# The weighing of the second attention's tiles, issued in two halves of 256 columns

## The chip, the cores and the metric

One core of a Trainium2 chip runs the whole program in one launch. The metric is the device time of that launch in microseconds (us). Six names stand for its engines in the profile: PE is the matmul engine and PEld its weight loads, DVE is VectorE, ACT is ScalarE, POOL is GpSimd and SP is SyncE, which issues the DMAs.

## The reference

The input is one sequence of 2048 tokens of 128 features. Four layers follow each other, each added to the stream after a layer norm: a windowed attention with a few global tokens, a memory lookup with a gate, a second attention, and a feed-forward layer with two chosen experts. The change is in the second attention alone:

```
q, k, v = heads of (x @ W.T + b)          # 16 heads of 8 features
q, k = rope(q, k)
scores = einsum('bhnd,bhmd->bhnm', q, k) / sqrt(8)
out = einsum('bhnm,bhmd->bhnd', softmax(scores), v)
```

In the reference the sequence counts as batch 1 here, so that each of the 16 heads has 2048 x 2048 scores.

## The kernel before

The second attention is `attn1_block`. A head is worked off in 16 steps (NT = 16), one for each tile of 128 keys, and a step has NC = 4 chunks of 512 queries. The loop `for s in range(STEPS): step(s)` runs over 16 x 16 = 256 steps, t = s % 16 being the step within its head. PE does three things in a step.

- **Scores** (`scores(c)`, L1090): one matmul of 64 rows by 512 columns for each chunk c. Its contraction takes partitions 0 to 63 for even heads and 64 to 127 for odd ones. Each result takes one of three PSUM banks in turn (TURNING), and waits in `free_bank` until ACT has read the score that was three before it. In the last head the ring has seven banks, since the banks of the row maxima are then free. ACT turns each result into `pb` (L1170, an exponential of 512 columns).
- **Row maxima of a later head** (`rows(g, n)`, L1053): one matmul of the same shape for each chunk, 64 + 12 units ahead of the scores. In steps 0 to 12 of a head this is the next head, which lies in the other half of the partitions; in steps 13 to 15 it is the head after next, in the same half as the scores. The matmuls fill four banks as two pairs, and DVE reduces each pair with one instruction (L1132, 1024 columns). The first matmul of a pair waits until DVE has reduced the pair that was there before:

```
if n % 2 == 0 and g * HALVES + u >= 2:
    pe.wait_ge(rows_reduced, g * HALVES + u - 1)
```

- **Weighing** (`weigh(h, t)`, L1078): the tile whose scores were made two steps earlier is multiplied with its values. The four chunks go to four groups of 32 output partitions of one bank (A_B), and work beside each other. Values and exponentials are float32, and the profile has two matmul records for each of the four. The bank collects the 16 tiles of a head, ACT then saves it as `acc` (L1161).

With S for a score, R for a row matmul and W for the weighing, the order that PE gets in a step is S0 R0 R1 S1 W S2 R2 S3 R3. R0 and R1 are one pair for DVE, R2 and R3 the other. In step 14 of a head the maxima of the next head are transposed right after W (L1068). The rows end at step 237 of 256, since the last head's maxima are complete there. PE issues in this order; where scores and rows lie in different halves of the partitions, their matmuls can run beside each other.

Of the kernel before, what the change touches and what calls it, by code (L numbers as in the profile page):

```python
# [17 lines left out]
NT = N // P  # L18
BANK = 512
NC = N // BANK  # L20
# [14 lines left out]
H1, HD1 = 16, 8  # L35
# [4 lines left out]
VCOLS = 32  # L40
# [883 lines left out]
def attn1_block(nc, m, a):  # L924

    SCALE = HD1 ** -0.5
    with ExitStack() as ctx:
        def sb(name, shape, dt=F32):
            return ctx.enter_context(nc.sbuf_tensor(name, shape, dt))

        def sem(name):
            return ctx.enter_context(nc.semaphore(name))
# [3 lines left out]
        VB = 3  # L936
        qf, kf = m.qf, m.kf
        vx = sb("vx", [P, VB, NT, VCOLS])
        pb = sb("pb", [P, 3, NC, BANK])
# [11 lines left out]
        st_ready, exp_ready, av_done = sem("st_ready"), sem("exp1_ready"), sem("av_done")  # L951
# [3 lines left out]
        M_B, A_B = 0, 6  # L955
        MAXIMA = (0, 1, 2, 3)
        TURNING = (4, 5, 7)
        UNITS = NT * NC
        HALVES = 2 * NT
        LEAD = 12  # L960
        STEPS = H1 * NT
        LOAD = 16 * 2 * PARTS
# [3 lines left out]
        def group(h):  # L966

            return h % 2 * HALFP

        def slot(h):  # L970
            return h // 2 % SLOTS

        def load_count(h):

            return (LOAD if h % 4 else 0) + (h // 4) * (LOAD + 16)
# [4 lines left out]
        def take(use, ring, reader, count):  # L980

            bank = ring[len(bank_of) % len(ring)]
            bank_of[use], freed_by[use] = bank, last_reader.get(bank, (rows_reduced, H1 * HALVES))
            last_reader[bank] = (reader, count)
# [54 lines left out]
        @block.tensor  # L1039
        def _(pe):  # L1040
            def rows(g, n):

                t, c, u = n // NC, n % NC, n // 2
                g0, b = group(g), slot(g)
                if n == 0 and g == 0:
                    pe.wait_ge(m.first_k, 16 * PARTS * NC)
                if g == 0 and n % UNITS_OF_CHUNK == 0:
                    pe.wait_ge(m.first_q[n // UNITS_OF_CHUNK], 16 * PARTS)
                if n == 0 and g:
                    pe.wait_ge(loaded[g % 4], load_count(g))  # L1050
                if n % 2 == 0 and g * HALVES + u >= 2:
                    pe.wait_ge(rows_reduced, g * HALVES + u - 1)
                mm = nc.tensor.matmul(m.psum[:, M_B + (u % 2) * 2 + n % 2, :], qf[g0:g0 + HALFP, b, t * P:(t + 1) * P],  # L1053
                                      kf[g0:g0 + HALFP, b, c * BANK:(c + 1) * BANK], start=True, stop=True)
                if n % 2:
                    mm.then_inc(rows_ready, 1)

            def free_bank(use):
                if freed_by[use]:
                    reader, count = freed_by[use]  # L1060
                    pe.wait_ge(reader, count)
                return bank_of[use]

            def turn_max(g):

                bank = free_bank(("max", g))
                pe.wait_ge(nparts_ready, g + 1)
                nc.tensor.transpose(m.psum[0:PARTS * NT, bank, 0:P], nparts[:, :].bitcast(F32), m.ident[:, :]).then_inc(nT_ready, 1)  # L1068

            def weigh(h, t):  # L1070

                pe.wait_ge(exp_ready, h * UNITS + (t + 1) * NC)
                if t == 0:
                    if h >= 1:
                        pe.wait_ge(acc_saved, h)
                    pe.wait_ge(vx_ready, h + 1)
                for c in range(NC):
                    mm = nc.tensor.matmul(m.psum[c * VCOLS:(c + 1) * VCOLS, A_B, :], vx[:, h % VB, t, :], pb[:, (h * NT + t) % 3, c, :],  # L1078
                                          start=(t == 0), stop=(t == NT - 1))
                mm.then_inc(av_done, 1)  # L1080

            def step(s):

                h, t = s // NT, s % NT
                g0, b = group(h), slot(h)
                if t == 0:
                    pe.wait_ge(max_rows_loaded, (h + 1) * 32)
                def scores(c):
                    bank = free_bank((s, c))
                    nc.tensor.matmul(m.psum[:, bank, :], kf[g0:g0 + HALFP, b, t * P:(t + 1) * P],  # L1090
                                     qf[g0:g0 + HALFP, b, c * BANK:(c + 1) * BANK], start=True, stop=True).then_inc(st_ready, 1)

                for c in range(NC):
                    n = UNITS + LEAD + s * NC + c
                    if c != 1:
                        scores(c)
                    if n < H1 * UNITS:
                        rows(n // UNITS, n % UNITS)
                    if c == 1:
                        scores(c)  # L1100
                        if s >= 2:
                            weigh((s - 2) // NT, (s - 2) % NT)
                        if t == NT - 2 and h + 1 < H1:
                            turn_max(h + 1)

            def keep_clock(g0):

                rows_of = slice(g0, g0 + HALFP)
                nc.tensor.matmul(m.psum[:, A_B if g0 else TURNING[1], :], m.fill[rows_of, 0:P], m.fill[rows_of, :],
                                 start=True, stop=True)  # L1110

            for n in range(UNITS):
                rows(0, n)
                keep_clock(HALFP)
            for n in range(LEAD):
                if n == 8:
                    turn_max(0)
                rows(1, n)
                keep_clock(0)
            for s in range(STEPS):  # L1120
                step(s)
            weigh(H1 - 1, NT - 2)
            weigh(H1 - 1, NT - 1)

        @block.vector
        def _(dve):

            def reduce_rows(v):

                g, u = v // HALVES, v % HALVES  # L1130
                dve.wait_ge(rows_ready, v + 1)
                nc.vector.tensor_reduce(rowmax[:, g % 2, u // 2, u % 2:u % 2 + 1],  # L1132
                                        m.psum[:, M_B + (u % 2) * 2:M_B + (u % 2) * 2 + 2, :].rearrange("p b c -> p (b c)"),
                                        AX_X, ALU.max).then_inc(rows_reduced, 1)

            def save_maxima(g):

                dve.wait_ge(rows_reduced, (g + 1) * HALVES)
                if g >= 1:
                    dve.wait_ge(nparts_ready, g)  # L1140
                nc.vector.tensor_reduce(nfull[:, :], rowmax[:, g % 2, :, :], AX_X, ALU.max, negate=True).then_inc(nmax_ready, 1)  # L1141

            for v in range(H1 * HALVES):
                reduce_rows(v)
# [291 lines left out]
def build(nc, a, out):  # L1436
    with ExitStack() as ctx:
# [61 lines left out]
        with ExitStack() as layer:  # L1499
            def lb(name, shape, dt=F32):  # L1500
                return layer.enter_context(nc.sbuf_tensor(name, shape, dt))

            m.qf, m.kf = lb("qf", [P, 2, N], F32R), lb("kf", [P, 2, N], F32R)
            m.fill = lb("fill", [P, BANK], F32R)
            m.parts = lb("parts", [P, 2, PARTS, N], F32R)
            m.stored = [layer.enter_context(nc.semaphore(f"parts_stored{i}")) for i in range(2)]
            m.first_k = layer.enter_context(nc.semaphore("first_k"))
            m.first_q = [layer.enter_context(nc.semaphore(f"first_q{c}")) for c in range(NC)]
            m.v1, m.attT, m.sums = lb("v1", [P, NT, D]), lb("attT", [P, N]), lb("sums", [P, BANK])
            memory_block(nc, m, a)  # L1510
            m.q_parts = nc.dram_tensor("q_parts", [PARTS, P, N], F32, kind="Internal").ap()
            m.k_parts = nc.dram_tensor("k_parts", [PARTS, P, N], F32, kind="Internal").ap()
            ln_block(nc, m, "ln2")
            project1_block(nc, m, a)
            attn1_block(nc, m, a)
            output1_block(nc, m, a)
# [46 lines left out]
```

## Time and profile before

| what | value |
|---|---|
| median of 3 runs | 1344.07 us (1342.58 to 1347.62) |
| profiled execution, its time | 1344.84 us |
| profiled execution, its span | 1343.1 us |
| mean granted TensorE clock | 0.967 of full speed |
| PE busy | 1267.1 us (94%) |
| DVE busy | 940.0 us (70%) |
| ACT busy | 860.9 us (64%) |
| score matmuls, first and last start | 535.0 and 1211.6 us |

The span reaches from the first to the last instruction of the profiled execution; 1.7 us of its time lie outside it. A busy PE is not a PE at its peak, since matmuls are pipelined and their ends are modelled. For that reason the starts of the matmuls say more than their durations. The second attention takes about half of the span, and it repeats itself: sixteen heads of sixteen steps.

### The profile page before, as it was taken

To read this page: it belongs to the slowest core of one execution; us is meant where nothing else is said; L and a number is where in the kernel's file an instruction comes from. 1 tells how busy PE (TensorE), PEld (TensorE's weight loads), DVE (VectorE), ACT (ScalarE), POOL (GpSimd) and SP (SyncE) were. 2 spreads that over 40 slices of the span, in tenths; PEclk is the share of its full clock that TensorE was granted. 3 is DMA by queue.
4 is the path that set the end of the run, shared out by engine and by line. 5 is a ranking of instruction groups with operands and counts; after the bars stand their busy time and mean duration, and the time that the engine had idled before them with its cause. 6 is when DMAs were issued, how large, how long until landed. Compare 5 with 4: busy or idle time off the path is not lost. (4 is left out here: it accounts for less than half of the span.)

```text
span 1343.1 us, 22401 instructions
## 1 busy us (share of the span) xinstructions
PE 1267.1 (94%) x8112; PEld 724.2 (54%) x8112; DVE 940.0 (70%) x1641; ACT 860.9 (64%) x2402; POOL 189.7 (14%) x365
## 2 busy tenths in 40 slices
PE   5999999999988867999999999999999999995898
PEld 4677777777855533444444444444444444433566
DVE  4566566666658879888888888888888888804200
ACT  1666666666747310777777877877778787792442
POOL 3233333333461120000000000000000000001100
PEclk8999999999998968999999999999999999997899
DMA  3200000000000030000000000000000000000101
GB/s 78 72 9 9 7 4 10 9 1 4 1 2 1 26 134 17 14 20 18 3 19 20 20 11 10 19 20 20 4 17 19 20 3 2 3 3 21 36 1 32
DMA packets 23100, 24.85 MB, mean 18 GB/s; under 512 B 7798, under 2 KB 17910, under 8 KB 21751
## 3 DMA queue, kind: packets, MB, share of 16 engines
q1 hardware_dynamic: 22990, 23.42, 5.5%
q8 instruction: 65, 1.06, 0.3%
q14 instruction: 45, 0.36, 0.1%
HBM read 16.52 MB, written 5.24 MB: 16 GB/s over the span
## 5 line engine op out<-in xcount | busy, mean ns | idle before, releaser
L1132 DVE TENSOR_REDUCE rowmax<-psum 128x1 f32<-128x1024 f32 x512 | 602.1, 1218 | 85.8 <-PE psum L1053 85.6
L1170 ACT ACTIVATE pb<-psum 128x512 f32<-128x512 f32 x1024 | 531.9, 604 | 123.1 <-PE psum L1090 120.1
L1090 PE MATMUL psum<-qf,kf 64*128 64x512 f32 x1024 | 374.1, 441 | 1.5 <-DMA qf<-nT 0.8
L1053 PE MATMUL psum<-kf,qf 64*128 64x512 f32 x1024 | 356.7, 446 | 11.2 <-DVE rowmax L1132 8.5
L1090 PEld LDWEIGHTS psum<-qf,kf 64*128 64x128 f32 x1024 | 171.2, 185 | 273.0 <-ACT pb L1170 252.7
L1078 PE MATMUL psum<-pb,vx 128*32 128x512 f32 x2048 | 273.6, 606 | 0.0
L1053 PEld LDWEIGHTS psum<-kf,qf 64*128 64x128 f32 x1024 | 162.9, 191 | 59.2 <-DVE rowmax L1132 32.8
L528 ACT ACTIVATE pr<-psum,nmax 128x128 f32<-128x128 f32 x256 | 93.7, 366 | 113.3 <-DVE nmax L471 113.2
L566 POOL TENSOR_TENSOR pr<-pr,rtotal 128x256 f32<-128x256 f32 (+1 forms) x256 | 110.5, 452 | 237.1 <-DVE rtotal L479 237.1
L470 DVE TENSOR_REDUCE nmax<-psum 128x2 f32<-128x256 f32 x128 | 53.6, 419 | 63.9 <-PE psum L339 63.1
L1195 POOL CAST nparts<-nfull 128x16 fp32r<-128x16 f32 x16 | 3.1, 197 | 668.0 <-DVE nfull L1141 668.0
L367 PE MATMUL psum<-pt,vz 128*128 128x128 f32 x512 | 78.1, 275 | 0.0
L1078 PEld LDWEIGHTS psum<-pb,vx 128*32 128x32 f32 x2048 | 40.3, 108 | 69.6 <-issue 38.3
L530 ACT ACTIVATE pr<-psum,nmax 128x32 f32<-128x32 f32 x256 | 72.9, 285 | 0.0
L335 PE MATMUL psum<-kx,qs 64*128 64x160 f32 x512 | 69.4, 348 | 1.7 <-ACT pr L530 1.7
L353 PE MATMUL psum<-ident,pr 128*128 128x128 f32 x384 | 70.0, 291 | 1.0 <-POOL pr L566 0.8
L485 DVE COPY pt<-psum 128x384 f32<-128x384 f32 x128 | 67.6, 528 | 1.7 <-PE psum L353 1.5
L367 PEld LDWEIGHTS psum<-pt,vz 128*128 128x128 f32 x512 | 67.5, 192 | 0.0
L335 PEld LDWEIGHTS psum<-kx,qs 64*128 64x128 f32 x512 | 38.6, 184 | 52.7 <-ACT pr L530 39.0
L1376 ACT ACTIVATE hT<-psum,b 128x512 f32<-128x512 f32 x48 | 33.0, 687 | 42.8 <-PE psum L1391 42.6
L530 ACT ACTIVATION_READ_ACCUMULATOR pr<-psum,nmax 128x1 f32 x256 | 52.8, 206 | 0.0
L365 PE MATMUL psum<-pt,gv 128*128 128x128 f32 x256 | 51.2, 282 | 0.3 <-ACT oT L538 0.2
(198 smaller groups left out, 1358.6 us busy)
## 6 DMA issues: line engine op xcount, KB each, us to landing
qf<-q_parts SPq DMA_DIRECT2D x30, 128.0 KB
kf<-k_parts SPq DMA_DIRECT2D x30, 128.0 KB
k_parts<-parts SPq DMA_DIRECT2D x4, 512.0 KB, 3.6
q_parts<-parts SPq DMA_DIRECT2D x4, 512.0 KB, 4.0
cos<-cos_table SPq DMA_DIRECT2D x1, 1024.0 KB, 5.1
sin<-sin_table SPq DMA_DIRECT2D x1, 1024.0 KB, 7.3
attT<-acc SPq DMA_DIRECT2D x64, 16.0 KB
sums<-acc SPq DMA_DIRECT2D x64, 2.0 KB
```

Source lines behind the costliest of these rows:

```text
L335: nc.tensor.matmul(m.psum[:, bank + j, 0:WL], qs[half[j], b, s * P:(s + 1) * P], kx[half[j], b, s, :], start=True, stop=False)
L353: mm = nc.tensor.transpose(m.psum[:, T_B, j * P:(j + 1) * P], pr[:, w % 4, j * P:(j + 1) * P], m.ident[:, :])
L367: mm = nc.tensor.matmul(ob, vz[:, b, j, s, :], pt[:, w % 2, j * P:(j + 1) * P], start=False, stop=(j == 1))
L485: nc.vector.tensor_copy(pt[:, w % 2, :], m.psum[:, T_B, 0:TW]).then_inc(pt_saved, 1)
L528: nc.scalar.activation(pr[:, i % 4, j * P:(j + 1) * P], sc[:, 0:P], ACT.Exp, bias=nmax[:, i % 4, j:j + 1], accum_out=total[:, i % 4, j:j + 1])
L530: mm = nc.scalar.activation(pr[:, i % 4, 2 * P + j * G0:2 * P + (j + 1) * G0], sc[:, P:WL], ACT.Exp, bias=nmax[:, i % 4, 2 + j:3 + j], acc ...
L566: mm = nc.gpsimd.tensor_tensor(prw, prw, rb, ALU.mult)
L1053: mm = nc.tensor.matmul(m.psum[:, M_B + (u % 2) * 2 + n % 2, :], qf[g0:g0 + HALFP, b, t * P:(t + 1) * P], kf[g0:g0 + HALFP, b, c * BANK:(c ...
L1078: mm = nc.tensor.matmul(m.psum[c * VCOLS:(c + 1) * VCOLS, A_B, :], vx[:, h % VB, t, :], pb[:, (h * NT + t) % 3, c, :], start=(t == 0), sto ...
L1090: nc.tensor.matmul(m.psum[:, bank, :], kf[g0:g0 + HALFP, b, t * P:(t + 1) * P], qf[g0:g0 + HALFP, b, c * BANK:(c + 1) * BANK], start=True, ...
L1132: nc.vector.tensor_reduce(rowmax[:, g % 2, u // 2, u % 2:u % 2 + 1], m.psum[:, M_B + (u % 2) * 2:M_B + (u % 2) * 2 + 2, :].rearrange("p b ...
L1170: nc.scalar.activation(pb[:, s % 3, c, :], m.psum[:, bank_of[(s, c)], :], ACT.Exp, scale=SCALE).then_inc(exp_ready, 1)
```

## The change

`weigh` gets a third argument, the part. For tiles 1 to 14 of a head it does columns 0 to 255 of each of the four chunks in part 0, and columns 256 to 511 in part 1. The first and the last tile of a head stay whole and are issued where part 1 is. Part 0 is issued between R0 and R1, part 1 where the whole weighing was. The order of a step is then S0 R0 Wa R1 S1 Wb S2 R2 S3 R3. Since the tile weighed in step t is that of step t - 2, the steps without a Wa are t = 1 and t = 2. The count of finished tiles (av_done) rises with part 1, and the wait for the exponentials stands at part 0.

```diff
+        HALF_B = BANK // 2
...
-            def weigh(h, t):
-
-                pe.wait_ge(exp_ready, h * UNITS + (t + 1) * NC)
+            def weigh(h, t, part):
+
+                whole = t == 0 or t == NT - 1
+                if part == 0 and whole:
+                    return
+                if part == 0 or whole:
+                    pe.wait_ge(exp_ready, h * UNITS + (t + 1) * NC)
                 if t == 0:
                     if h >= 1:
                         pe.wait_ge(acc_saved, h)
                     pe.wait_ge(vx_ready, h + 1)
+                cols = slice(part * HALF_B, (part + 1) * HALF_B) if not whole else slice(0, BANK)
                 for c in range(NC):
-                    mm = nc.tensor.matmul(m.psum[c * VCOLS:(c + 1) * VCOLS, A_B, :], vx[:, h % VB, t, :], pb[:, (h * NT + t) % 3, c, :],
-                                          start=(t == 0), stop=(t == NT - 1))
-                mm.then_inc(av_done, 1)
+                    mm = nc.tensor.matmul(m.psum[c * VCOLS:(c + 1) * VCOLS, A_B, cols], vx[:, h % VB, t, :],
+                                          pb[:, (h * NT + t) % 3, c, cols], start=(t == 0), stop=(t == NT - 1))
+                if part == 1:
+                    mm.then_inc(av_done, 1)
...
                 for c in range(NC):
                     n = UNITS + LEAD + s * NC + c
+                    if c == 1 and s >= 2:
+                        weigh((s - 2) // NT, (s - 2) % NT, 0)
                     if c != 1:
                         scores(c)
...
                     if c == 1:
                         scores(c)
                         if s >= 2:
-                            weigh((s - 2) // NT, (s - 2) % NT)
+                            weigh((s - 2) // NT, (s - 2) % NT, 1)
...
-            weigh(H1 - 1, NT - 2)
-            weigh(H1 - 1, NT - 1)
+            for t in (NT - 2, NT - 1):
+                for part in range(2):
+                    weigh(H1 - 1, t, part)
```

## Rows read from the trace of the kernel before

**Rows 1.** Windows: stretch in us, each engine's busy us and records, clock, DMA share, GB/s

```profile
786.00:829.00 43.00, 42.93 (x262) 19.00 (x258) 37.86 (x34) 34.09 (x67) 0.88 (x4) 1.00 0.05 16
...
1173.00:1214.00 41.00, 40.59 (x233) 14.91 (x232) 0.00 (x0) 38.35 (x76) 0.00 (x0) 1.00 0.01 3
```

**Rows 2.** Waits, 580 to 1160 us: in total us, times, longest us

```profile
PEld psum L1090 <- ACT pb L1170: 218.0, 367, 0.8
ACT pb L1170 <- PE psum L1090: 105.6, 190, 0.8
```

**Rows 3.** Timeline of one step: start us, length us, engine, line, names, count, idle before

```profile
864.07 0.49 PE L1090 MATMUL psum<-qf,kf 64*128 64x512 f32 x1
...
864.40 0.39 PE L1090 MATMUL psum<-qf,kf 64*128 64x512 f32 x1
...
864.40 0.39 PE L1053 MATMUL psum<-kf,qf 64*128 64x512 f32 x1
864.60 2.06 ACT L1170 ACTIVATE pb<-psum 128x512 f32<-128x512 f32 x4 [0.54 <-PE psum L1090]
864.64 0.39 PE L1090 MATMUL psum<-qf,kf 64*128 64x512 f32 x1
...
864.68 0.73 PE L1053 MATMUL psum<-kf,qf 64*128 64x512 f32 x2
864.87 2.36 DVE L1132 TENSOR_REDUCE rowmax<-psum 128x1 f32<-128x1024 f32 x2 [0.24 <-PE psum L1053]
...
865.25 0.49 PE L1090 MATMUL psum<-qf,kf 64*128 64x512 f32 x1
...
865.67 1.07 PE L1078 MATMUL psum<-pb,vx 128*32 128x512 f32 x8
866.66 0.18 PEld L1090 LDWEIGHTS psum<-qf,kf 64*128 64x128 f32 x1 [0.84 <-ACT pb L1170]
866.67 0.49 PE L1090 MATMUL psum<-qf,kf 64*128 64x512 f32 x1
...
867.28 0.73 PE L1053 MATMUL psum<-kf,qf 64*128 64x512 f32 x2
...
867.85 0.49 PE L1090 MATMUL psum<-qf,kf 64*128 64x512 f32 x1
```

**Rows 4.** Timeline of the same step, cut closer so that merged records part

```profile
864.87 1.22 DVE L1132 TENSOR_REDUCE rowmax<-psum 128x1 f32<-128x1024 f32 x1 [0.24 <-PE psum L1053]
865.01 0.39 PE L1053 MATMUL psum<-kf,qf 64*128 64x512 f32 x1
```

**Rows 5.** All instructions of line 1170: min, median, max ns

```profile
L1170 ACT ACTIVATE pb<-psum x1024: 591/598/740, 535.6 to 1212.3; 128x512 f32<-128x512 f32 x171
```

**Rows 6.** Chain that ended last, in the experts: start us, us, count

```profile
1273.55 10.30 PE psum L1391 x24
1283.86 10.72 PE psum L1400 x96
```

**Rows 7.** Timeline of PE, step 13 of a head

```profile
870.07 0.63 PE L1053 MATMUL psum<-kf,qf 64*128 64x512 f32 x2
870.54 0.40 PE L1090 MATMUL psum<-qf,kf 64*128 64x512 f32 x1
870.87 1.07 PE L1078 MATMUL psum<-pb,vx 128*32 128x512 f32 x8
```

**Rows 8.** Timeline of PE in the last head, without row matmuls

```profile
1180.71 1.06 PE L1078 MATMUL psum<-pb,vx 128*32 128x512 f32 x8
1181.70 1.19 PE L1090 MATMUL psum<-qf,kf 64*128 64x512 f32 x4
1182.82 1.06 PE L1078 MATMUL psum<-pb,vx 128*32 128x512 f32 x8
```

**Rows 9.** Timeline of POOL: one such cast in every head

```profile
785.78 0.20 POOL L1195 CAST nparts<-nfull 128x16 fp32r<-128x16 f32 x1 [42.00 <-DVE nfull L1141]
...
828.68 0.20 POOL L1195 CAST nparts<-nfull 128x16 fp32r<-128x16 f32 x1 [41.99 <-DVE nfull L1141]
```

## Prediction

> **What bounds the kernel now.** I read the windows first, to see whether the stage that the change touches has one limit or several. In a stretch of 43 us, one head, PE is busy for 42.9 us, DVE for 37.9 and ACT for 34.1, at the full granted clock; in the last head DVE has nothing to do and PE still fills its time [rows 1]. PE's number is no proof, since its records overlap. The waits are more telling: ACT waits for scores and the scores' weight loads wait for ACT [rows 2]. Two engines that wait for each other form a loop, so the timeline of one step has to say how long each loop is.
>
> The step repeats every 2.60 us: S2 starts at 864.07 and again at 866.67 [rows 3]. Three things take part in it.
>
> - The loop of the exponentials. S2 starts at 864.07, ACT takes it 0.53 later (864.60), needs 0.60 [rows 5], and 0.05 later S1 starts in the bank that this frees (865.25). W follows 0.42 later, the next S2 1.00 after it [rows 3]. That is 0.53 + 0.60 + 0.05 + 0.42 + 1.00 = 2.60, the whole step. This is the binding loop.
> - The loop of the row maxima. R0 starts at 864.68 and R1 at 865.01, 0.33 later [rows 3, 4]. R1 lasts 0.39, DVE could start 0.07 after its end (R3: 864.40 + 0.39 to 864.87) and needs 1.22 [rows 3, 4]. The next R0 comes 0.05 after DVE has ended: 864.87 + 2.36 = 867.23, against 867.28 [rows 3]. R0 to R0 is thus at least 0.33 + 0.39 + 0.07 + 1.22 + 0.05 = 2.06. It has some 0.5 us to spare, which DVE now spends on the pair before.
> - PE alone. S0 to R0, R1 and S1 has one small gap for DVE and one for ACT, so that PE's own pace is close behind both.
>
> **What the change does to a step.** It removes nothing; it adds four matmuls (eight records of weights and eight of matmuls), and moves half of the columns to a place between R0 and R1. No DMA is issued elsewhere, and av_done rises where it did. The added wait for exponentials is met: the tile was finished two steps earlier. Behind it queue R1 and S1, and that is the point.
>
> *Price of a half.* A whole weighing takes 1.00 us from its start to the next score [rows 3], with two records of 512 columns behind each other in each group. The nearest rows for the columns are the float32 matmuls of the experts, 24 records of 512 columns in 10.30 us and 96 of 128 in 10.72 [rows 6]: 0.429 and 0.112 each, 0.83 ns for a column. Twice 256 columns fewer are 0.42 us less, so a half costs 1.00 - 0.42 = 0.58; I take 0.57, as the start of the first group already holds its weight load. The lower bound is 0.43, the columns alone (512 x 0.83 ns); the upper one 0.66, where the fixed part of the whole, 1.00 - 0.85 = 0.15, is half as large again in a half. That a record's length counted for nothing (1.00) is excluded by the experts' rows.
>
> *Price of getting in.* From a late R0 to Wa I take the 0.42 that S1 needs before W, and 0.33 where the matmul in front of it was not late (870.54 to 870.87) [rows 3, 7]. A matmul that follows one of its kind costs 0.23 (864.40 to 864.64) [rows 3].
>
> *Price of getting out.* After W the next matmul lasts 0.49 in place of 0.39, since its weights are loaded only then: load at 866.66, matmul at 866.67 [rows 3]. R1 is now such a matmul. The Trainium skill, page TensorE: Matmul & The Clock Gate, section Step-by-step: what each phase is for, says that the engine pulls weight loads ahead of matmuls in flight where the row groups don't conflict or the load goes to the background buffer. Were that so for R1 behind Wa, 0.10 would fall out of each added switch; the row shows that it is not so behind W.
>
> Now the loop of the maxima is R0, Wa, R1, DVE, R0: 0.42 + 0.57 + (0.49 + 0.07) + 1.22 + 0.05 = 2.82. R1 is 0.66 us later behind its R0 than before, and these banks can't be refilled until DVE has read the pair. This is longer than the 2.60 of the step, so it becomes the limit. The loop of the exponentials relaxes (S1 starts 1 us or more after it could), and S1 starts beside R1, in the other half of the partitions. PE alone would need, from R0 on: 0.33 + 0.57 + 0 + 0.42 + 0.57 + 0.33 + 0.24 = 2.46. It waits the rest before R0. DVE is busy 2.36 of 2.82, no limit. So a common step goes from 2.60 to 2.82, 0.22 more.
>
> **The sum.** Heads repeat every 42.90 us [rows 9].
>
> - Steps 3 to 12 of a head are of this kind, nine distances between their R0. The rows run until step 13 of the fifteenth head, so 15 x 9 x 0.22 = 29.7 us.
> - At a head's end (steps 13 to 15, and 0 of the next) rows and scores share a half and follow each other at 0.23. Here PE itself is the limit, and a step pays the added switches: two halves for one whole 2 x 0.57 - 1.00 = 0.14; R0 to Wa 0.33 in place of R0 to R1 0.23, 0.10; the cold R1 0.10. That is 0.34 in each of the three steps from 13 to 0, 0.10 more in step 13 (its R0 is late), and some 0.2 around them (DVE's loop in step 0, and the entry to step 13). Steps 1 and 2, with whole tiles, stay. 1.3 us for a head, 14 times: 18.2.
> - Behind the rows' end, a step takes 2.11 us (1180.71 to 1182.82) [rows 8], PE at its own pace, ACT 4 x 0.60 with overlap below it. Each of the 16 halved tiles there pays 0.14 + 0.10 + 0.10 = 0.33: 5.3 us.
>
> Together 53 us on the profiled execution's 1344.8, that is 1398.0. Its time is 0.8 above the median of the runs. I predict 1398; half a per cent, about 6.7 us, is what a measurement of this kernel can tell from no change.
>
> **Rivals.**
>
> 1. *The maxima loop as worked out* (0.66): 1398, between 1388 and 1410.
> 2. *Dearer switches* (0.13). A second switch in so short a distance may cost more than the one that the trace shows. With 0.05 more for each half, the loop is 2.87 and the sum 135 x 0.27 + 14 x 1.7 + 16 x 0.43 = 67: 1412. With 0.66 for a half it is 1425 or more. Against it: all the switches shown cost the same.
> 3. *Weights loaded ahead* (0.09). R1's weights come in while Wa streams, R1 is not cold, and the loop is 2.72: 135 x 0.12 = 16, ends 14 x 0.9 = 13, last part 16 x 0.23 = 4, together 33: 1377. The load row behind W speaks against it [rows 3]. The rule of the Trainium skill named above (TensorE: Matmul & The Clock Gate) would have it so.
> 4. *R0 isn't held* (0.07): the pair of banks has more slack than I read from the code, so that PE's own 2.46 is the step. It gains 135 x 0.14 = 19, and the ends and the last part cost 18 + 5: 1349, no change. The 0.05 between DVE's end and R0 speaks against it [rows 3].
> 5. *The other side, faster* (0.05): the step now loses time because W stands in one piece in ACT's loop (ACT idles 0.54 in each step [rows 3]). If a half cost its columns alone, with drain and cold loads beside other work, the maxima loop is 0.23 + 0.43 + 0.39 + 0.07 + 1.22 + 0.05 = 2.39, and a step gains up to 0.2: 135 x 0.2 = 27, some 1317. It decides from the point at which the added half takes less than 0.35 between R0 and R1 (0.57 - 0.22), which is less than its columns.
>
> The page TensorEngine Tiling (Array Packing) of the Trainium skill, section Key Properties, states that a change of the tiling mode drains the engine. It speaks against this change, which doubles the changes in a step; without any drain the sum would be that of rival 5. The 0.42 into W and the cold matmul behind it agree with the page [rows 3].
>
> **How the numbers follow.** The range has to hold rival 1 and most of 2 and 3: 1376 to 1414. Outside are 4 and 5 and a part of 2, some 0.17. Faster by over 0.5% is rival 5, 0.05; within 0.5% is rival 4 with a remainder, 0.06; slower 0.89.
>
> **What would show it.** In the timeline after: Wa some 0.42 behind R0, R1 0.57 behind Wa, S1 beside R1; S2 to S2 2.82; R0 0.05 behind DVE's end, with PE idle before it, DVE starting some 0.07 behind R1's end; more waiting of L1053 for rowmax. A head of some 46 us, and 2.44 for a step of the last head. Wrong would be: R1 closer than 0.9 behind R0, a maxima loop that has slack while the step is short, or a weighing half that takes clearly other than 0.57.

## The result and the profile after

The changed kernel takes 1396.43 us (median of 4 runs, 1392.87 to 1398.17), the kernel before 1345.40 us beside it (4 runs, 1342.58 to 1347.62). The ratio is 1.037, with a 95% interval from 1.0346 to 1.0394: slower by 51 us. Predicted were 1398, between 1376 and 1414.

The first view to read is the timeline of a common step, the one that answers to the step shown of before [rows 3]. Score matmuls are now L1097, rows L1054, the weighing L1084, DVE's reduce L1142 and ACT's exponential L1180. The columns are start, length, engine, line, names, shapes, count, and the idle time before.

```profile
881.78 0.39 PE L1097 MATMUL psum<-qf,kf 64*128 64x512 f32 x1
...
882.02 0.50 PE L1054 MATMUL psum<-kf,qf 64*128 64x512 f32 x1
...
882.45 0.64 PE L1084 MATMUL psum<-pb,vx 128*32 128x256 f32 x8
883.01 0.18 PEld L1054 LDWEIGHTS psum<-kf,qf 64*128 64x128 f32 x1 [0.41 <-issue]
883.02 0.50 PE L1054 MATMUL psum<-kf,qf 64*128 64x512 f32 x1
...
883.02 0.50 PE L1097 MATMUL psum<-qf,kf 64*128 64x512 f32 x1
...
883.45 0.64 PE L1084 MATMUL psum<-pb,vx 128*32 128x256 f32 x8
883.55 2.49 DVE L1142 TENSOR_REDUCE rowmax<-psum 128x1 f32<-128x1024 f32 x2 [0.31 <-PE psum L1054]
...
884.02 0.49 PE L1097 MATMUL psum<-qf,kf 64*128 64x512 f32 x1
...
884.35 0.39 PE L1097 MATMUL psum<-qf,kf 64*128 64x512 f32 x1
...
884.59 0.39 PE L1097 MATMUL psum<-qf,kf 64*128 64x512 f32 x1
884.83 0.18 PEld L1054 LDWEIGHTS psum<-kf,qf 64*128 64x128 f32 x1 [0.29 <-DVE rowmax L1142]
884.83 0.49 PE L1054 MATMUL psum<-kf,qf 64*128 64x512 f32 x1
```

R0 starts at 882.02, Wa at 882.45, R1 and S1 side by side at 883.02, and DVE takes the pair 0.53 later. One reduce lasts 1.22 us, so it ends at 883.55 + 1.22 = 884.77 (the 2.49 of the line covers two reduces), and the next R0 starts at 884.83. The weight load of R0 names its releaser: rowmax, by DVE, after 0.29 us of idle time. From R0 to R0 that is 2.81 us, made of 0.43 + 0.57 + 0.53 + 1.22 + 0.06. S0 was issued 0.24 earlier (884.59) and did not have to wait. The weights of R1 come at 883.01, with the matmul, and it lasts 0.50 where a matmul whose weights came earlier lasts 0.39. Such a matmul is called cold here; before, the one behind the whole weighing was the same.

The waits between 580 and 1160 us say how the limit changed hands: engine and line, what it waited for, us in total, times, longest us. First before, then after:

```profile
PEld psum L1053 <- DVE rowmax L1132: 7.1, 14, 0.5
```

```profile
PEld psum L1054 <- DVE rowmax L1142: 36.4, 126, 0.3
PEld psum L1097 <- ACT pb L1180: 32.0, 52, 0.8
```

The rows' weight loads wait for DVE 126 times in place of 14, and those of the scores wait 32.0 us for ACT in place of 218.0 [rows 2].

The heads follow each other in this rhythm; the same POOL cast as in [rows 9], one in each head:

```profile
805.36 0.20 POOL L1205 CAST nparts<-nfull 128x16 fp32r<-128x16 f32 x1 [45.22 <-DVE nfull L1151]
...
851.43 0.20 POOL L1205 CAST nparts<-nfull 128x16 fp32r<-128x16 f32 x1 [45.16 <-DVE nfull L1151]
```

46.07 us in place of 42.90. The page gives the stage in groups; columns are busy us and mean ns, then the idle time before and what ended it:

```profile
L1142 DVE TENSOR_REDUCE rowmax<-psum 128x1 f32<-128x1024 f32 x512 | 622.7, 1224 | 113.7 <-PE psum L1054 106.8
L1180 ACT ACTIVATE pb<-psum 128x512 f32<-128x512 f32 x1024 | 550.8, 599 | 163.2 <-PE psum L1097 161.7
L1054 PE MATMUL psum<-kf,qf 64*128 64x512 f32 x1024 | 436.7, 478 | 5.8 <-DVE rowmax L1142 3.9
...
L1084 PE MATMUL psum<-pb,vx 128*32 128x256 f32 (+1 forms) x3840 | 321.0, 406 | 0.0
```

The rows' matmuls last 478 ns in the mean (446 before), as R1 is a cold one now, and the weighing has 3840 records for 2048. DVE's and ACT's own work per instruction is as it was; both only wait longer.

Where did the time go? Three windows each, before and after: the stretch of rows ahead of the first step, the steps with rows, and the steps behind them.

```profile
488.30:535.00 46.70, 37.37 (x153) 16.23 (x153) 43.54 (x39) 1.55 (x2) 3.05 (x7) 0.70 0.07 26
535.00:1169.90 634.90, 633.87 (x3788) 279.85 (x3790) 558.69 (x488) 502.40 (x974) 11.21 (x41) 0.99 0.04 14
1170.00:1214.00 44.00, 43.37 (x249) 15.84 (x245) 1.54 (x3) 40.69 (x80) 0.42 (x2) 1.00 0.01 3
```

```profile
487.20:536.00 48.80, 44.21 (x153) 19.46 (x153) 44.31 (x39) 1.55 (x2) 3.02 (x7) 0.50 0.07 25
536.00:1218.30 682.30, 682.27 (x5438) 294.63 (x5439) 579.53 (x488) 521.14 (x974) 11.25 (x41) 0.99 0.04 13
1218.30:1267.00 48.70, 48.51 (x393) 18.87 (x389) 1.81 (x3) 41.01 (x81) 0.42 (x2) 1.00 0.02 3
```

The steps with rows grew from 634.9 to 682.3 us, 47.4. The steps behind them grew by 4.4: from the last row matmul to the save of the last head's bank it is 44.2 us before (1169.9 to 1214.1) and 48.6 after (1218.3 to 1266.9). The stretch ahead, which the change doesn't touch, took 46.7 at a mean granted clock of 0.70 and 48.8 at 0.50, and is part of the difference of these two executions only. The two spans differ by 53.3, the medians of the runs by 51.0.

### The profile page after: what moved, and what is told of

Read it like the earlier page. It is cut to its first block and busy times, and to the rows that moved or that the text cites. A ratio compares the mean times of both kernels' runs of the same rounds, so it can differ in the third digit from the quotient of the medians.

```text
span 1396.4 us, 25985 instructions
## 1 busy us (share of the span) xinstructions
PE 1328.8 (95%) x9904; PEld 747.2 (54%) x9904; DVE 960.5 (69%) x1641; ACT 880.6 (63%) x2402; POOL 190.1 (14%) x365
## 5 line engine op out<-in xcount | busy, mean ns | idle before, releaser
L1142 DVE TENSOR_REDUCE rowmax<-psum 128x1 f32<-128x1024 f32 x512 | 622.7, 1224 | 113.7 <-PE psum L1054 106.8
L1180 ACT ACTIVATE pb<-psum 128x512 f32<-128x512 f32 x1024 | 550.8, 599 | 163.2 <-PE psum L1097 161.7
L1054 PE MATMUL psum<-kf,qf 64*128 64x512 f32 x1024 | 436.7, 478 | 5.8 <-DVE rowmax L1142 3.9
L1097 PE MATMUL psum<-qf,kf 64*128 64x512 f32 x1024 | 379.7, 444 | 0.7 <-DMA qf<-nT 0.7
L1084 PE MATMUL psum<-pb,vx 128*32 128x256 f32 (+1 forms) x3840 | 321.0, 406 | 0.0
L1054 PEld LDWEIGHTS psum<-kf,qf 64*128 64x128 f32 x1024 | 177.9, 195 | 168.5 <-issue 95.7
L1097 PEld LDWEIGHTS psum<-qf,kf 64*128 64x128 f32 x1024 | 172.7, 185 | 142.3 <-issue 75.8
L1084 PEld LDWEIGHTS psum<-pb,vx 128*32 128x32 f32 x3840 | 75.7, 108 | 130.2 <-issue 84.2
L1386 ACT ACTIVATE hT<-psum,b 128x512 f32<-128x512 f32 x48 | 33.0, 687 | 43.2 <-PE psum L1401 42.9
```

What stands on the lines that cost most here:

```text
L1180: nc.scalar.activation(pb[:, s % 3, c, :], m.psum[:, bank_of[(s, c)], :], ACT.Exp, scale=SCALE).then_inc(exp_ready, 1)
```

## The experiments

All times are medians, each with the ratio to the kernel before in runs on the same chip. Before took 1345.9 us beside e1 to e4, 1345.1 beside e5 to e7, and 1346.2 beside e8 to e10.

| kernel | order of a common step | us | ratio (95%) | step forecast | step measured |
|---|---|---|---|---|---|
| after | S0 R0 Wa R1 S1 Wb S2 R2 S3 R3 | 1396.4 | 1.037 (1.0346 to 1.0394) | 2.82 | 2.81 |
| e1 | S0 R0 R1 S1 Wb S2 R2 S3 R3 Wa | 1347.6 | 1.0013 (1.0000 to 1.0027) | 2.47 | 2.46 |
| e2 | as e1, tiles 1 to 10 only | 1330.6 | 0.9882 (0.9863 to 0.9901) | 2.47 | 2.46 |
| e3 | S0 R0 R1 S1 Wa Wb S2 R2 S3 R3 | 1348.0 | 1.0018 (1.0008 to 1.0028) | 2.60 to 2.63 | 2.61 |
| e4 | S0 Wa R0 R1 S1 Wb S2 R2 S3 R3 | 1382.2 | 1.0261 (1.0243 to 1.0280) | 2.70 | 2.69 |
| e5 | as after, tiles 1 to 10 only | 1380.5 | 1.0253 (1.0224 to 1.0282) | 2.81 | 2.81 |
| e6 | as after, short reduce | 1326.4 | 0.9872 (0.9849 to 0.9895) | 2.46 | 2.46 |
| e7 | as before, short reduce | 1326.2 | 0.9859 (0.9839 to 0.9878) | 2.60 | 2.60 |
| e8 | S0 R0 R1 S1 S2 R2 S3 R3 W | 1370.7 | 1.0172 (1.0140 to 1.0204) | 2.60 | 2.67 |
| e9 | as e2, whole in the last head | 1329.1 | 0.9871 (0.9847 to 0.9895) | 2.47 | 2.47 |
| e10 | S0 R0 W R1 S1 S2 R2 S3 R3 | 1459.3 | 1.0842 (1.0808 to 1.0875) | 3.25 | 3.23 |

The step is the distance from S0 to S0, read from the starts of the score matmuls in steps 4 to 12 of a head. Where an expectation names no step (e5, e9), its forecast here is the one that its sum uses.

**e1: the first half between the pairs.** The rival to a loop is that a second half costs PE its time anywhere. So the half was kept and its place changed.

```diff
             def step(s):
 
+                if s >= 2:
+                    weigh((s - 2) // NT, (s - 2) % NT, 0)
                 h, t = s // NT, s % NT
...
-                    if c == 1 and s >= 2:
-                        weigh((s - 2) // NT, (s - 2) % NT, 0)
```

> The first half Wa is issued between R3 and S0, so no weighing stands between R0 and R1. Theory of the maxima loop: R0 to R1 is 0.33 again, the loop drops under the step, and a common step is PE's own path: S2 to S3 0.33, to Wa 0.33, to S0 0.57, R0 to R1 0.33, to Wb 0.33, to S2 0.57 = 2.47. 135 x 0.13 gained, against some 1.1 x 14 at the heads' ends and 5 behind the rows' end: about 3 us over before, 1347. Rival, that a second half costs PE's time wherever it stands: as after, some 1397.

```profile
860.34 0.50 PE L1099 MATMUL psum<-qf,kf 64*128 64x512 f32 x1
...
860.67 0.39 PE L1099 MATMUL psum<-qf,kf 64*128 64x512 f32 x1
...
861.00 0.64 PE L1084 MATMUL psum<-pb,vx 128*32 128x256 f32 x8
861.57 0.18 PEld L1099 LDWEIGHTS psum<-qf,kf 64*128 64x128 f32 x1 [0.41 <-ACT pb L1180]
...
861.91 0.39 PE L1099 MATMUL psum<-qf,kf 64*128 64x512 f32 x1
...
862.24 0.64 PE L1084 MATMUL psum<-pb,vx 128*32 128x256 f32 x8
862.80 0.18 PEld L1099 LDWEIGHTS psum<-qf,kf 64*128 64x128 f32 x1 [0.41 <-ACT pb L1180]
```

S2 860.34, S3 860.67, Wa 861.00, S0 861.57, S1 861.91, Wb 862.24, S2 862.80: 2.46 us, each term within 0.01 of its forecast. The kernel is 49 us faster than after with the same matmuls and the same number of switches into and out of the weighing. In a common step the loss of the change isn't that it halves, but where the half stands.

**e4: the first half one matmul earlier**, before R0 in place of behind it.

```diff
-                    if c == 1 and s >= 2:
-                        weigh((s - 2) // NT, (s - 2) % NT, 0)
                     if c != 1:
                         scores(c)
+                    if c == 0 and s >= 2:
+                        weigh((s - 2) // NT, (s - 2) % NT, 0)
```

> Wa is moved by one matmul, from behind R0 to before it: S0 Wa R0 R1 S1 Wb. Maxima loop: R0 to R1 0.33 again, loop 2.1, so a common step is PE's path: S2 to S3 0.33, to S0 0.24, to Wa 0.33, to R0 0.57, to R1 0.33, to Wb 0.33, to S2 0.57 = 2.70. 135 x 0.10 = 14, ends 17, behind the rows 5: 1380, 17 under after. Rival, that only the number of switches counts: no difference from after, 1397.

1382.2 and a step of 2.69: 14 us under after. By the sums of both, what is left against e1 is S0, which stands alone here, without R0 beside it, and takes 0.23 of its own (S3 starts at 863.89, S0 at 864.12 in its trace); 2.70 and 2.47 were forecast, 2.69 and 2.46 measured.

**e10: the whole weighing inside the pair.** This takes the kernel before, adds no record and, in a common step, no switch, and makes the distance from R0 to R1 longer. In step 14 of a head it does add one, since the transposition of the maxima no longer stands behind a weighing. (The first and the last tile of a head stay where they were, as in the change.)

```diff
                     if c != 1:
                         scores(c)
+                    if c == 1 and s >= 2 and (s - 2) % NT not in (0, NT - 1):
+                        weigh((s - 2) // NT, (s - 2) % NT)
...
-                        if s >= 2:
+                        if s >= 2 and (s - 2) % NT in (0, NT - 1):
                             weigh((s - 2) // NT, (s - 2) % NT)
```

> Kernel before, with the whole weighing of tiles 1 to 14 moved between R0 and R1. No switch of tiling and no record is added. Maxima loop: 0.42 + 1.00 + 0.56 + 1.22 + 0.05 = 3.25 for the common step: 135 x 0.65 = 88, and some 8 for step 0 of each head: 1441. Rival, that the loss comes from the number of switches and records: no change, 1345.

```profile
860.81 0.50 PE L1053 MATMUL psum<-kf,qf 64*128 64x512 f32 x1
...
861.24 1.06 PE L1078 MATMUL psum<-pb,vx 128*32 128x512 f32 x8
...
862.23 0.49 PE L1053 MATMUL psum<-kf,qf 64*128 64x512 f32 x1
...
862.76 2.36 DVE L1134 TENSOR_REDUCE rowmax<-psum 128x1 f32<-128x1024 f32 x2 [0.88 <-PE psum L1053]
...
864.04 0.50 PE L1053 MATMUL psum<-kf,qf 64*128 64x512 f32 x1
```

R0 at 860.81, W 861.24, R1 862.23, DVE 862.76, the next R0 at 864.04: 3.23 where 3.25 was forecast. The total is 18 us over the forecast of 1441. A head takes 50.5 us, 7.6 more than before: the nine distances give 9 x 0.63 = 5.7, the heads' ends the rest. There I had counted 0.5 a head, and it was 1.9; over half of that lies in steps 13 to 15. The moved weighing and the switch of the transposition are likely reasons; no run parts them.

**e6 and e7: a shorter reduce.** DVE reads only the first of the two banks of a pair; half of the scores are left out of the row maxima. If the maxima loop is the limit of after, it must vanish with the reduce, and before must not care.

```diff
-                                        m.psum[:, M_B + (u % 2) * 2:M_B + (u % 2) * 2 + 2, :].rearrange("p b c -> p (b c)"),
+                                        m.psum[:, M_B + (u % 2) * 2:M_B + (u % 2) * 2 + 1, :].rearrange("p b c -> p (b c)"),
```

> The changed kernel, with DVE reading only the first of the two banks of a pair (512 of 1024 columns; half of the scores are left out of the row maxima). The reduce falls from 1.22 to about 0.65 us, the maxima loop from 2.81 to 2.25, and the common step to PE's own 2.46: 47 us under after, about 1350. Rival, that PE's added switches are the limit: no change from after, 1397.

> The kernel before with the same short reduce (512 of 1024 columns read). Its step is held by the loop of the exponentials, 2.60, and its maxima loop had 0.5 to spare: no change, 1344, within 5 us. If DVE held the step of before, it falls clearly.

Both totals missed, by 24 and 18 us. The windows tell why, first of e6 and then of e7, and behind them the reduce of e7 in DVE's groups (600 to 700 us; busy us, mean ns):

```profile
486.90:518.20 31.30, 27.69 (x153) 12.57 (x153) 25.77 (x39) 1.55 (x2) 3.08 (x7) 0.94 0.10 39
518.20:1147.10 628.90, 627.50 (x5438) 263.09 (x5439) 327.17 (x487) 509.44 (x974) 11.24 (x41) 1.00 0.05 14
```

```profile
491.50:522.90 31.40, 26.11 (x153) 12.66 (x153) 24.78 (x39) 1.55 (x2) 3.12 (x7) 0.95 0.10 39
522.90:1155.20 632.30, 630.78 (x3788) 261.93 (x3790) 310.41 (x487) 503.18 (x974) 11.30 (x41) 1.00 0.04 14
```

```profile
L1132 DVE TENSOR_REDUCE rowmax<-psum 128x1 f32<-128x512 f32 x74 | 48.5, 688 | 51.2 <-PE psum L1053 51.2
```

The stretch ahead of the first step, which no expectation had counted, is DVE's: 43.5 of 46.7 us busy before, and with the short reduce it takes 31.4 us. That is 15.3 us of what e7 gained, and 17.5 of what e6 gained over after. (The granted clock of this stretch was 0.95 in e7 and 0.70 before, so the shorter reduce and the higher clock are not parted there; among the traces with the full reduce the stretch differs by only 2 us between 0.50 and 0.70.) In the steps with rows e7 is 2.6 us below before, 632.3 against 634.9; 2.0 of that lie in steps 1 and 2 of the first head, and the common step is 2.60: before is not held by DVE there. In e6 the same steps fall from 682.3 to 628.9 us, 53 in place of the 47 forecast, and the step is PE's own 2.46, the same as in e1. So with a reduce of 0.69 us the halves make a common step 0.14 shorter than the whole weighing does (2.46 in e6, 2.60 in e7); with one of 1.22 they make it 0.21 longer. That e6 is no faster than e7 all the same (1326.4 and 1326.2) is the price of the halves at the heads' ends and in the last head. This also measures rival 4 of the prediction: 2.46 is what the step would be if R0 weren't held.

**e3: both halves in the old place**, for the price of smaller records alone: part 0 is issued directly before part 1.

> Both halves are issued where the whole was, one behind the other, with no change of tiling between them. If the price of a half lies in getting in and out (0.15 of its 0.57) and in the place, the smaller records alone cost 0.03 each step or less: up to 6 us over before, 1344 to 1350. Rival, that smaller records cost by themselves (0.09 for a half): 0.18 x 224 = 40 us over, 1384.

```profile
881.66 1.07 PE L1084 MATMUL psum<-pb,vx 128*32 128x256 f32 x16
882.66 0.49 PE L1097 MATMUL psum<-qf,kf 64*128 64x512 f32 x1
```

Sixteen records take the 1.00 us from their start to the next score that eight longer ones took [rows 3]. The kernel is 2.4 us slower than before by the ratio (1.1 to 3.8 by the interval). Halving without an added switch is nearly free.

**e5: the change in the middle of a head only.** One line differs from after:

```diff
-                whole = t == 0 or t == NT - 1
+                whole = not 1 <= t <= 10
```

> The change in its own place, but only for tiles 1 to 10 of a head (steps 3 to 12). By the sum: 135 x 0.21 = 28 us, and a little at the entry: 1372 to 1375. If the heads' ends and the last head carried more of the loss than 23 us, it would be well below 1370.

1380.5, 35 us over before, above the 27 to 30 that I had set. A head takes 44.8 us, 1.9 more than before, as expected. Forgotten were the ten tiles of the last head, which are halved too: the steps behind the rows take 47.6 us in place of 44.2, 3.4 more. The steps with rows grew by 30.4 in its trace; the rest is within what the runs of this kernel scatter (1374.8 to 1385.1). So of the loss of after some 35 us belong to tiles 1 to 10 of the sixteen heads, and some 16 to the tiles 11 to 14; with this scatter the split is rough.

**e2 and e9: the better place, where it gains.** e2 is e1 with the line of e5; e9 keeps the last head whole as well, with this line:

```diff
-                whole = t == 0 or t == NT - 1
+                whole = not 1 <= t <= 10 or h == H1 - 1
```

> As the one with Wa between R3 and S0, but only tiles 1 to 10 of a head are halved (steps 3 to 12, where rows and scores lie in different halves of the partitions); the others stay whole. Theory of the maxima loop: the gain of 0.13 in each of 135 distances stays and the ends cost nothing: 17 us under before, 1327. Rival, that the place doesn't matter: 28 us over before, 1372.

> The version with Wa between R3 and S0 and halves for tiles 1 to 10 only, now whole in the last head too, where no rows run. It should give back the 3.4 us that the ten halved tiles of the last head cost (10 x 0.33): 18 us under before, 1327, a ratio of 0.986. If the last head's extra doesn't come from the halves, it stays at 0.988.

e2 is 15 us faster than before (17 forecast), e9 17 (18 forecast). The steps behind the rows take 47.6 us in e2 and 44.2 in e9, as forecast; the medians (1330.6 and 1329.1) don't separate the two. A head takes 41.7 us against 42.9. Both are faster than the kernel before and the changed one, with intervals clear of 1.

**e8: the whole weighing between the pairs**, to see whether the place alone had gained it: the edit of e10, with the weighing issued at the head of `step`.

> Kernel before, with the whole weighing of tiles 1 to 14 moved between R3 and S0. The loop of the exponentials then runs from S0 over ACT to S3 and the weighing, with the same terms: 0.53 + 0.60 + 0.05 + 0.42 + 1.00 = 2.60. Theory: no change, 1345 within 5 us; what the halves between the pairs gained came from the halving, which takes 0.43 out of this loop. Rival, that the place between the pairs gave it (S1 beside R1 again): 15 us under before, 1330.

```profile
862.46 1.06 PE L1078 MATMUL psum<-pb,vx 128*32 128x512 f32 x8
...
863.45 0.50 PE L1092 MATMUL psum<-qf,kf 64*128 64x512 f32 x1
...
864.04 2.06 ACT L1172 ACTIVATE pb<-psum 128x512 f32<-128x512 f32 x4 [0.61 <-PE psum L1092]
...
864.70 0.50 PE L1092 MATMUL psum<-qf,kf 64*128 64x512 f32 x1 [0.25 <-ACT pb L1172]
...
865.13 1.07 PE L1078 MATMUL psum<-pb,vx 128*32 128x512 f32 x8
```

The place alone gains nothing, as forecast; but it loses 25 us, which was not, so this forecast (no change within 5 us) missed. The loop of the exponentials is there: S0 at 863.45, ACT at 864.04, S3 at 864.70 in the bank that this frees, W at 865.13. It is 0.59 + 0.60 + 0.06 + 0.43 + 0.99 = 2.67. The new 0.06 lies between S0 and its exponential, which comes 0.59 behind the score and not 0.53. The exponential of chunk 0 has a second wait in the program (av_done), on a count long reached. The kept traces agree with that as far as they go: where ACT was idle, the exponential of chunk 0 started 0.10 us behind the end of its matmul in e1, e2, e8 and e9, and that of chunk 2, which has one wait, 0.04 in each of them. No run took the second wait away, so the cause is not shown. Nine steps of 0.07 give 0.6 of the 1.5 us that a head is longer. Another 0.27 is step 14 (3.26 to 3.53), where the transposition now needs a change of tiling of its own:

```profile
888.64 0.39 PE L1092 MATMUL psum<-qf,kf 64*128 64x512 f32 x1
888.97 0.28 PE L1068 MATMUL psum<-ident,nparts 128*32 128x128 f32 x1
889.18 0.50 PE L1092 MATMUL psum<-qf,kf 64*128 64x512 f32 x1
```

From S at 888.64 over the transposition to the next S 0.54 us pass, where two scores in a row need 0.23. The remaining 0.6 of a head lies nearly all between step 15 and step 3 of the next head, around the two whole tiles that stayed in their old place; its cause is open.

## Why the prediction was right

- *The limit of before* was taken to be the loop of the exponentials, with the maxima loop 0.5 us below it. The runs agree: a reduce half as long leaves the step at 2.60 (e7), so it isn't DVE; two halves in the old place keep it (e3), and the whole weighing elsewhere still stands in this loop (e8). In the trace S1 starts 0.05 behind ACT in each common step [rows 3]. No run shortens the exponential itself, so that this loop and nothing else binds rests on its sum of 2.60 and on these.
- *The maxima loop becomes the limit.* Shown from three sides: shorter distance from R0 to R1 (e1, e4), longer distance without any halving (e10), shorter reduce (e6). Its size was 2.82 by the sum and 2.81 in the trace. DVE started 0.53 behind the start of a cold R1 in place of 0.56, the other terms were within 0.01.
- *A half costs 0.57.* Measured 0.57 (882.45 to 883.02). The way from the experts' matmuls of 128 and 512 columns to one of 256 held: it gave 0.58, and the 0.01 taken off it had no row behind it, but is too small to decide anything.
- *Cold matmuls behind a weighing.* R1 lasts 0.50 and its weights come with it; rival 3 (1377), which the rule on weight loads that the prediction names from the Trainium skill (TensorE: Matmul & The Clock Gate) would have allowed, did not happen, and rival 2 (dearer switches, 1412) didn't either.
- *The sum.* Forecast 29.7 + 18.2 = 47.9 for the steps with rows, measured 47.4. The parts agree too: nine distances of 0.21 in a head, and 1.3 at its end as forecast, though there two small errors cancel. Step 0 is 0.33 longer, more than the 0.2 left for everything around the three steps, and steps 1 and 3 are 0.09 shorter each, which nothing in the sum foresaw. Behind the rows 5.3 were forecast and 4.4 measured. A halved step there is 2.45 in place of 2.11, 0.34 as the sum had it (0.33), in steps 3 to 15 of the last head, and step 0 grows as much (2.21 to 2.55). But steps 13 and 14 of the fifteenth head, which I had counted as dearer, are shorter: 2.45 and 2.67 after, 2.61 and 2.81 before. On the medians the forecast is 2 us too high, within the runs' scatter; that it is so close is in part luck, as the stretch ahead of the first step alone moves by 2 us from one execution to the next.
- *Rival 5, the faster side*, had the right loss in view, the weighing in one piece in ACT's loop, and the wrong price for this place: the gain exists (a common step of 2.46 in e1, and a faster kernel in e2 and e9), once the half stands between two pairs.

What was incomplete is my picture of the stages around: the stretch ahead of the first step, where DVE is busy for 43.5 of 46.7 us, entered neither e6 nor e7, and the heads' ends were off in e8 and e10.

## What to carry to other kernels

Before a piece of work is split and a part of it moved, write down every loop of engines through the place of insertion, with its slack, and compare with the smallest slack what the insertion adds to that loop. Here the loop of the maxima had 0.54 us to spare (2.60 - 2.06), and the insertion added 0.76: R1 comes 0.66 later behind R0, and being cold it lasts 0.10 longer. The difference is the 0.22 of the forecast. Between two matmuls that fill one buffer for another engine, the piece also delays the time at which that buffer comes free. With the first half two matmuls earlier, between two such pairs, the common step is shorter than before (2.46 to 2.60), and with tiles 1 to 10 alone halved so is the whole kernel.

## What was not expected of the hardware

- An added exit from a weighing need not be lost time. R1 and S1 were 0.24 apart before, since S1 waited for ACT; behind Wa they start together (883.02 both). With two switches in a step where there was one, the step is 2.46 in e1 and e6, below the 2.60 of before. By the sums this is the loop of the exponentials giving way, as only half of the weighing is left in it; how fast PE alone would have been before was not measured.
- Sixteen short records in four output groups take the same 1.00 us as eight of double length (e3).
- The same stretch of row matmuls ahead of the first step took 46.7 us in two traces, whose mean granted clock there was 0.70 (at the lower level, 1.2 GHz, until some 19 us before its end, then at the upper, 2.4 GHz), and 48.4 to 48.9 in the eight others with the full reduce, at 0.50 to 0.52: some 2 us that belong to no edit.
